# Self-attention: the value projection moved and cut into blocks of 128 tokens

## The reference

```python
q = (x @ wq + bq).reshape(Bq, Nq, H, HD)
k = (ctx @ wk + bk).reshape(Bq, Nk, H, HD)
v = (ctx @ wv + bv).reshape(Bq, Nk, H, HD)
scores = jnp.einsum('bqhd,bkhd->bhqk', q, k) / np.sqrt(HD)
...
attn = jax.nn.softmax(scores.astype(jnp.float32), axis=-1).astype(scores.dtype)
out = jnp.einsum('bhqk,bkhd->bqhd', attn, v).reshape(Bq, Nq, D)
```

## Time and profile before

| | us |
|---|---|
| median of 3 runs | 3801.18 |
| lowest and highest run | 3792.87, 3816.62 |
| profiled execution | 3808.84 |
| its span, first to last instruction | 3807.1 |
| TensorE busy (matmuls) | 3435.5 (90%) |
| VectorE busy | 2225.9 (58%) |
| ScalarE busy | 2328.3 (61%) |
| POOL busy | 830.8 (22%) |
| mean granted TensorE clock, 1 is 2.4 GHz | 0.964 |

### The profile page before, as it was taken

The page is one execution under the profiler, slowest core; times in us unless marked ns, Lnnn a source line. Parts: engine busy times, 40 slices in busy tenths (PEclk is TensorE's granted clock), DMA queues, the critical chain, the costliest instruction groups (busy, mean ns, idle before and its releaser), DMA issues.

```text
span 3807.1 us, 59346 instructions
## 1 busy us (share of the span) xinstructions
PE 3435.5 (90%) x22289; PEld 2018.6 (53%) x22289; DVE 2225.9 (58%) x3509; ACT 2328.3 (61%) x4071; POOL 830.8 (22%) x546
## 2 busy tenths in 40 slices
PE   8999998998999888988998889988988899899988
PEld 6777875435644654446435744365446443564465
DVE  3334335865496557943875559536945487549654
ACT  2333334776587646874785558765874578657764
POOL 0322223004400511034003410051014100340051
PEclk8999999999999999999999999999999999999999
DMA  5001002000000001001000010000000100000000
GB/s 173 7 29 35 6 29 88 2 12 24 27 2 12 12 21 36 2 24 38 2 2 13 12 56 2 21 26 16 2 13 12 56 1 13 24 27 2 6 19 13
DMA packets 73089, 87.17 MB, mean 23 GB/s; under 512 B 11823, under 2 KB 62578, under 8 KB 72694
## 3 DMA queue, kind: packets, MB, share of 16 engines
q1 hardware_dynamic: 47846, 63.23, 5.1%
q10 hardware_dynamic: 24976, 20.15, 1.7%
HBM read 72.49 MB, written 9.56 MB: 22 GB/s over the span
## 4 chain that ended last, share of the span: by engine, by line
PE 74%; DVE 13%; ACT 9%; issue 2%; POOL 2%; DMA 0%; SPq 0%; ACTq 0%; DVEq 0%; POOLq 0%
PE ps L671 69%; ACT probs L1396 5%; DVE mxh L1711 5%; PE ps L1114 3%; DVE ctxk L1660 2%; DVE ow L1726 1%; PE ps L977 1%; DVE tok L1446 1%; DVE small L1430 1%; DVE x L1677 1%; DVE mx L1708 1%; POOL hidl L1812 1%; ACT ow L1402 1%; POOL small L1748 1%; ACT qs L1363 1%
## 5 line engine op out<-in xcount | busy, mean ns | idle before, releaser
L1396 ACT ACTIVATE probs<-ps 128x512 f32<-128x512 f32 (+1 forms) x2176 | 1220.9, 635 | 307.0 <-PE ps L671 262.4
L1711 DVE TENSOR_REDUCE mxh<-ps 128x2 f32<-128x1024 f32 x1024 | 1212.6, 1219 | 158.9 <-PE ps L671 155.6
L671 PE MATMUL ps<-probs,v 128*32 128x256 f32 (+2 forms) x7616 | 732.7, 457 | 6.3 <-ACT probs L1396 6.3
L671 PE MATMUL ps<-ks,qs 64*128 64x512 f32 x2048 | 483.9, 481 | 63.2 <-DVE mxh L1711 46.4
L1748 POOL TENSOR_TENSOR small<-small 128x4 f32<-128x4 f32 x66 | 67.7, 1026 | 2036.4 <-DVE small L1440 2036.4
L671 PE MATMUL ps<-qs,ks 64*128 64x512 f32 x2048 | 457.9, 428 | 4.1 <-DVE mxh L1711 3.0
L671 PEld LDWEIGHTS ps<-ks,qs 64*128 64x128 f32 x2048 | 193.3, 184 | 424.7 <-issue 301.5
L671 PEld LDWEIGHTS ps<-qs,ks 64*128 64x128 f32 x2048 | 249.5, 187 | 189.2 <-ACT probs L1396 138.2
L671 PEld LDWEIGHTS ps<-probs,v 128*32 128x32 f32 (+1 forms) x7616 | 150.6, 108 | 276.2 <-ACT probs L1396 205.8
L671 PE MATMUL ps<-hT,slot 128*128 128x512 f32 x448 | 232.5, 652 | 21.7 <-issue 8.5
L1708 DVE TENSOR_REDUCE mx<-ps 128x4 f32<-128x312 f32 x384 | 165.9, 477 | 143.2 <-PE ps L671 140.0
(11 more groups left out here) (219 smaller groups left out, 5942.3 us busy)
## 6 DMA issues: line engine op xcount, KB each, us to landing
slot<-in_L_w SPq DMA_DIRECT2D x8, 1024.0 KB, 10.4
slot<-in_L_fc_w SPq DMA_DIRECT2D x8, 1024.0 KB, 5.4
xin<-in_x ACTq DMA_DIRECT2D x5, 1024.0 KB, 6.0
x_after_block<-x ACTq DMA_DIRECT2D x20, 256.0 KB, 2.4
xin<-x_after_block SPq DMA_DIRECT2D x5, 1024.0 KB, 5.5
ew<-in_L_e_w SPq DMA_DIRECT2D x6, 768.0 KB, 14.2
x<-in_x ACTq DMA_DIRECT2D x4, 1024.0 KB, 7.2
qs<-mrow SPq DMA_DIRECT2D x256, 2.0 KB
```

What stands on the lines that cost most here:

```text
L671: return pe.matmul(out, lhsT, rhs, start=start, stop=stop)
L1396: ins = act.activation(dst, src, ACT.Exp, scale=SCALE)
L1711: dve.tensor_reduce(mxh[:, z, t, j // 2, j % 2, :], ps[:, a:a + 2, :], AX.X, ALU.max, negate=True).then_inc(dve_done, M.add(dve_done, name))
```

## The change

("V", t) now stands for one block of 128 tokens instead of a pair. Blocks 0 and 1 stand in the lead-in where pair 0 stood, blocks 2 to 5 take the four empty entries of `beside`, block 6 stands in unit 1 and block 7 in unit 3 (counted from 0). Each has a bank and a copy by ScalarE (128x256) of its own. A PV waits for the block that it reads.

```diff
-            ("K", "dddd", "q", 0, 0), ("K", "aaaa", "k", 0, 0), ("P", "k", 0, 1), ("P", "q", 0, 1), ("V", 0), ("K", "ddaa", "k", 0, 1), *[("mask",)] * first)
+            ("K", "dddd", "q", 0, 0), ("K", "aaaa", "k", 0, 0), ("P", "k", 0, 1), ("P", "q", 0, 1), ("V", 0), ("V", 1), ("K", "ddaa", "k", 0, 1), *[("mask",)] * first)
...
+        values = [("V", t) for t in range(2, NT - 2)]
...
-                  + [w for k in halves("q", 1, 0, "A") + halves("q", 1, 1, "A") for w in (k, None)] + halves("k", 1, 1, "A"))
+                  + [w for k in halves("q", 1, 0, "A") + halves("q", 1, 1, "A") for w in (k, values.pop(0))] + halves("k", 1, 1, "A"))
...
-            if u < 3:
-                put(tag, ("V", u + 1))
+            if u in (1, 3):
+                put(tag, ("V", NT - 2 + u // 2))
...
-                        t2 = step[1]
+                        t = step[1]
                         b, act_was, dve_was = take(name, act=name, banks=single())
-                        pe.wait_ge(act_done, upto(act_done, *((ln, "hT", t2 // 2, k) for k in range(KC)), *act_was))
+                        pe.wait_ge(act_done, upto(act_done, *((ln, "hT", t // TPH, k) for k in range(KC)), *act_was))
                         pe.wait_ge(dve_done, upto(dve_done, *dve_was))
-                        for i in range(1 if cross else 2):
-                            t = 2 * t2 + i
-                            for k in range(KC):
-                                ins = mm(ps[0:kw, b, i * D:(i + 1) * D], src[:, k, t * P:t * P + kw], wv[:, k, :], k == 0, k == KC - 1)
+                        for k in range(KC):
+                            ins = mm(ps[0:kw, b, 0:D], src[:, k, t * P:t * P + kw], wv[:, k, :], k == 0, k == KC - 1)
...
-                        pe.wait_ge(act_done, upto(act_done, (tag, "S", g, n, kt, GH - (2 if cross else 1)), (tag, "V", 0 if cross else kt // 2), *act_was))
+                        pe.wait_ge(act_done, upto(act_done, (tag, "S", g, n, kt, GH - (2 if cross else 1)), (tag, "V", kt), *act_was))
...
-                        t2, i = step[1], 1 if cross else 2
-                        src = ps[0:kw, M.where(name), 0:i * D].rearrange("p (i h d) -> p i h d", i=i, d=HD)
+                        t = step[1]
+                        src = ps[0:kw, M.where(name), 0:D].rearrange("p (h d) -> p h d", d=HD)
                         act.wait_ge(mm_done, upto(mm_done, name))
-                        act.activation(v[0:kw, 2 * t2:2 * t2 + i, :, 0:HD], src, ACT.Copy).then_inc(act_done, M.add(act_done, name))
+                        act.activation(v[0:kw, t, :, 0:HD], src, ACT.Copy).then_inc(act_done, M.add(act_done, name))
```

## The result

The changed kernel is slower: the ratio of its runs to those of before is 1.0066, with a 95% interval from 1.0042 to 1.0091. Its median is 3836.4 us (six runs, 3830.1 to 3837.1), that of before 3798.7 us (six runs). The forecast was 3797 us in a range from 3777 to 3815, so the time lies above it. The profiled execution has a span of 3828.7 us for 3807.1. The two medians are 37.7 us apart, more than the ratio says: the six runs of before fall into two groups, four from 3792.9 to 3801.2 us and two near 3817, so their median moves easily.

A forecast was written before the change was run, and what follows sets the result against it. TensorE was taken to bound most of the chain, VectorE the lead-in's second part. Lead-in 2.52 us longer against units shortened gave 0.5 us gained in each of eight self-attentions, -4.0 us: 3797 us, range 3777 to 3815.

The forecast's parts named there:

- The reading of before: Lead-in: TensorE alone until 1021.9 us, then VectorE sets the pace, 2.26 us a turn, TensorE having 0.3 us to spare.
- Blocks 0 and 1: Start of the lead-in, pair 0's place: same TensorE cost, ScalarE copies 0.16 us more beside idle time, nothing on the path.
- Blocks 2 to 5: Four lead-in turns become TensorE-bound at 2.96 us each; M comes 2.27 us later, first scores 2.52 us later.
- Units 0 to 3: After the lead-in: three pairs leave, two blocks enter; unit 4 starts 0.67 us early, 0.5 us gained per stage taken.
- The bounds: Work moved from units to lead-in, 3.86 us a stage: were either place free, -31 or +31 us, within 1%.
- The rule weighed: Short TensorE idle times make its clock swing; a lead-in without waits would gain up to 2.5 us more in the slow stage.
- rival 3: TensorE's clock: slow stage keeps pace, 2.5 us more gained (3794.5), or two more stages slow, 5 us lost (3802); chance 0.10.
- Rivals 1 and 2: Lead-in: VectorE's pace hides the values, 3779 us, chance 0.18; or the lead-in pays in full, 3807 us, chance 0.16.
- rival 2: Lead-in: the four blocks find no cover, scores 3.88 us late, +0.7 us a stage, 3807 us; chance 0.16.
- The signs: Lead-in maxima stand singly, M some 2.3 us later, VectorE's long waits in units under 1 us, steady part half a microsecond early.
- the steady half unit: From unit 4 on: 1.24 us of TensorE against one maximum of 1.155, in either kernel, so the advance is carried on.

The follow-up runs named there:

- cut_only: Against the kernel before: values cut into blocks of 128 tokens with own bank and copy, all left at the old places; 3821.4 us, ratio 1.0023.
- early: Against the changed kernel: blocks 6 and 7 stand in units 0 and 1 instead of 1 and 3; 3812.9 us, ratio 1.0005 to before.
- first_pair: Against the kernel before: only unit 0 emptied, blocks 2 and 3 in the lead-in's first and third place, 4 to 7 paired in units 1 and 2; 3842.7 us, 1.0107.
- both_in_first: Against the changed kernel: blocks 6 and 7 both in unit 0, none in later units; 3847.2 us, ratio 1.0110 to before.

## Why the prediction was wrong

**The reading of before was right.** VectorE's pace in the lead-in, TensorE's in its place once the blocks were there, and the DMA between M's row and the scores (3.79 us now, 3.81 forecast from) came out.

**Blocks 0 and 1** cost 0.1 us at most (`cut_only`: 26.4 for 26.3); the 128x256 copy takes 0.38 us, as taken from the 77x256 one.

**Blocks 2 to 5** were sized at +2.52 us on the first scores and measured +2.80. The turn is 3.05 us, not 2.96: a block costs 1.07 between two tiles (1022.78 to 1023.85), not the 0.97 that is half of a pair's 1.93. That is 4 x 0.1 at M, and 0.3 us at the first scores, some 2 us in all.

**Units 0 to 3** is the step that failed. It took every duration from matmuls at 2.4 GHz, priced the units at -1.15, -0.49, -1.84 and +0.29 us against before, and so took 3.2 us off. Measured in the stage that was read are -0.96, +1.05, -0.59 and +0.69 us, 0.2 us *more* than before, as TensorE was at 1.2 GHz from inside unit 0 to inside unit 2. Over the eight stages the distance is 28.05 us on average for my 25.0, which is 8 x 3.05 = 24 us, and the lead-in of the sixth stage adds 1.6. With the forecast's -4 and the 2 us of the lead-in that makes -4 + 2 + 24 + 2 = +24 us, and 25 us is what the ratio gives. `early`, with the same two blocks in units 0 and 1, has 24.6 to 24.7 us, so the sum itself is good to half a microsecond when the clock holds.

**The bounds** (no more than 31 us either way, so within 1%) rested on the same assumption. The ratio of the change stays within 1%, but by no merit of the bound: `first_pair`, which moves less work, has 1.0107 (1.0067 to 1.0146). A fall of the clock can cost more than the work that was moved.

**The rule weighed, and rival 3.** I had the rule in hand. The Trainium skill (TensorE: Matmul & The Clock Gate, section "A second HAM failure mode: psum-queue depth-cycling") says that short idle times between groups of matmuls make the clock swing; the trace of the changed kernel agrees, with 0.50 over 7 us behind a stretch in which TensorE was busy 3.99 us. But before has such idle times too (busy 4.63 us of 7) at a clock of 1.00, so the rule alone does not say where the clock falls. Two things went wrong. I asked only what the denser lead-in would gain, not what the emptied units would lose, and I argued from seven stages with full clock that the waits are harmless. They were, with the value pairs between them. And the size: rival 3 had 2.5 us in two stages more, where it was 3 us in all eight, six of them between 3.2 and 4.2.

**Rivals 1 and 2** did not come about; scores 0 came 2.8 us late, below the 3.2 from which rival 2 was to decide. The kernel did get slower, as rival 2 had it, but not for its reason; that is luck. The signs by which I wanted to tell held for the lead-in; the long waits of VectorE did not shrink (2.31 us was the longest, as 2.24 before), and the steady half unit is 1.23 us for the 1.24 of the forecast (1060.58 to 1061.81).

## What to carry to other kernels

Before work is moved out of a stretch in which TensorE already waits, ask what the stretch looks like without it: matmuls beside a wait may cost no time and yet hold the clock or bring it back, and once it falls, the matmuls behind take up to twice as long (a value block 2.08 us for 1.13). A sum over matmuls holds only as long as the granted clock of each stretch is that of the rows it was taken from; an unread matmul in the gap is a cheap experiment to find out. And values put into a VectorE-bound loop cost 0.7 us each in every turn, and 0.28 or 0.6 each in every second one, depending on which turns these are.

## What was not expected of the hardware

Over the 28 us from M's row on, TensorE is busy 22.27 us before and 22.30 after, by the eight rows above. That is not the same work: matmuls at the lower clock are busy for longer, and the rows count 152 of them before and 137 after. So a busy share does not show that the clock has fallen.

Nor did it foretell a fall. These are the 7 us ahead of a fall in `both_in_first` and, of the same length, the thinnest stretch of the stage of before that was read, where the clock held:

```profile
1037.78:1044.78 7.00, 4.89 (x23) 3.01 (x23) 5.10 (x6) 4.34 (x9) 0.00 (x0) 1.00 0.01 3
1033.34:1040.34 7.00, 4.16 (x22) 2.54 (x21) 4.94 (x5) 4.51 (x7) 0.00 (x0) 1.00 0.01 1
```

Where the work stood did tell: the change and `early` have the same instructions in another order, and the clock fell in all eight stages of one and in none of the other. What sets a fall off exactly is left open. Some (with the first scores, in the lead-in) came and went from stage to stage and with the execution, and no run here was made to tell what they hang on.
